# Attention scores from float32r parts in 48 and 50 rows, with TensorE's attention program written out

## The reference

```python
Q = (x @ Wq + bq)   # 32 heads of 16;  K, V: 8 heads of 16, each shared by 4 query heads
scores = einsum('bhqd,bhkd->bhqk', Q, K) / sqrt(16)
out = einsum('bhqk,bhkd->bhqd', softmax(scores), V)  @ Wo + bo
# moe: top 2 of 8 experts of 512x512 for each token, weights = softmax of the two gate logits
```

## Time and profile before

| | |
|---|---|
| median of 3 runs | 1973.47 us (1973.37 to 1979.02) |
| profiled execution: first to last instruction | 1974.0 us |
| profiled execution, own time | not given apart from the span; the span lies 0.5 us over the median |
| mean granted TensorE clock | 0.967 |
| TensorE (matmuls) busy | 1827.0 us, 93% |
| VectorE, ScalarE, GpSimd busy | 73%, 61%, 10% |
| rounds of attention | about 140 to 1632 us |

### The profile page before, as it was taken

The page is one execution under the profiler, slowest core; times in us unless marked ns, Lnnn a source line. Parts: engine busy times, 40 slices in busy tenths (PEclk is TensorE's granted clock), DMA queues, the critical chain, the costliest instruction groups (busy, mean ns, idle before and its releaser), DMA issues.

```text
span 1974.0 us, 35320 instructions
## 1 busy us (share of the span) xinstructions
PE 1827.0 (93%) x9850; PEld 684.5 (35%) x9851; DVE 1436.3 (73%) x1599; ACT 1203.5 (61%) x2291; POOL 204.3 (10%) x220
## 2 busy tenths in 40 slices
PE   6997999999999999999999999999999988857980
PEld 3532333333333333333333333333333216625870
DVE  4495888888888888888888888888888705562214
ACT  2334777777777777777777777777777783322330
POOL 4443120000000000000000000000000004051006
PEclk9998999999999999999999999999999998967995
DMA  5226330100100000001000100100000004034548
GB/s 180 82 74 113 130 113 18 33 11 14 32 11 11 11 32 11 11 11 32 11 11 18 33 11 14 32 3 3 3 24 3 25 4 151 1 133 149 165 138 255
DMA packets 77019, 104.49 MB, mean 53 GB/s; under 512 B 28072, under 2 KB 49592, under 8 KB 76992
## 3 DMA queue, kind: packets, MB, share of 16 engines
q1 hardware_dynamic: 62624, 61.37, 10.8%
q0 software_dynamic: 11920, 40.93, 6.0%
q10 hardware_dynamic: 2448, 1.84, 0.4%
HBM read 58.49 MB, written 45.22 MB: 53 GB/s over the span
## 4 chain that ended last, share of the span: by engine, by line
PE 87%; DVE 3%; POOL 3%; DMA 2%; issue 2%; ACT 1%; ACTq 0%; SPq 0%; DVEq 0%; POOLq 0%
PE bank L805 25%; PE bank L773 24%; PE bank L799 22%; PE bank L902 7%; PE bank L744 3%; DVE max_kc L1093 2%; DMA arena_q<-q_parts 1%; POOL slots_x L411 1%; PE bank L817 1%; PE bank L979 1%; POOL ys L420 1%; POOL xs L420 1%; PE bank L759 1%; ACT arena_p L639 1%; PE bank L929 1%
## 5 line engine op out<-in xcount | busy, mean ns | idle before, releaser
L1093 DVE TENSOR_REDUCE max_kc<-bank 128x1 f32<-128x1024 f32 x1024 | 1212.0, 1219 | 207.7 <-PE bank L773 201.2
L639 ACT ACTIVATE arena_p<-bank 128x512 f32<-128x512 f32 x2048 | 1057.5, 603 | 406.3 <-PE bank L799 402.4
L799 PE MATMUL bank<-arena_q,arena_k 99*128 (+1 forms) x2048 | 617.2, 379 | 22.1 <-DMA arena_q<-q_parts 14.0
L773 PE MATMUL bank<-arena_k,arena_q 96*128 (+1 forms) x2048 | 614.7, 381 | 3.4 <-DVE max_kc L1093 3.1
L805 PE MATMUL bank<-arena_p,v_cur 128*32 128x512 f32 x4096 | 546.0, 605 | 0.7 <-ACT arena_p L639 0.7
L773 PEld LDWEIGHTS bank<-arena_k,arena_q 96*128 (+1 forms) x2048 | 161.7, 97 | 501.4 <-issue 337.9
L799 PEld LDWEIGHTS bank<-arena_q,arena_k 99*128 (+1 forms) x2048 | 196.7, 97 | 394.0 <-ACT arena_p L639 159.4
L805 PEld LDWEIGHTS bank<-arena_p,v_cur 128*32 128x32 f32 x4096 | 80.6, 108 | 125.2 <-issue 109.9
L353 POOL COPY v_cur<-v_all 128x256 f32 (+1 forms) x8 | 3.2, 399 | 1159.3 <-PE bank L805 1159.2
L1245 DVE TENSOR_TENSOR x2T_lo<-bank,x2T_hi 128x512 fp32r<-128x512 f32 x39 | 27.0, 692 | 106.0 <-ACT x2T_hi L646 106.0
L744 PE MATMUL bank<-xT,arena_p 128*128 128x512 f32 x160 | 75.6, 594 | 2.8 <-ACT xT L587 2.8
(11 more groups left out here) (153 smaller groups left out, 883.0 us busy)
## 6 DMA issues: line engine op xcount, KB each, us to landing
arena_q<-q_parts SPq DMA_DIRECT2D x192, 64.0 KB, 2.3
slots_x<-be_sb POOLq DMA_DIRECT2D x39, 256.0 KB, 2.3
xs<-slots_x SPq DMA_DIRECT2D x39, 256.0 KB, 2.7
slots_y<-ys SPq DMA_DIRECT2D x39, 256.0 KB, 2.0
we_raw<-in_L_ffn_expert_w POOLq DMA_DIRECT2D x8, 1024.0 KB, 6.1
q_parts<-arena_k SPq DMA_DIRECT2D x16, 384.0 KB, 3.0
heads_out<-o_norm SPq DMA_DIRECT2D x33, 128.0 KB, 2.3
at<-heads_out SPq DMA_DIRECT2D x4, 1024.0 KB, 6.6
```

The costliest lines, as they stand in the source:

```text
L639: act.activation(probs[:, u % PRING, :], bank[:, ring_bank(("score", u)), :], ACT.Exp, scale=SCALE).then_inc(p_ready, 1)
L773: mm = pe.matmul(bank[:, 2 + 2 * (m % 2) + q, :], q_flat[0:CROW, bass.ds(qo, P)], k_flat[0:CROW, bass.ds((j // NC) * T + (2 * half + q) * ...
L799: pe.matmul(bank[:, ring_bank(("score", u)), :], k_flat[0:SROW, bass.ds((i // NC) * T + kt * P, P)], q_flat[0:SROW, bass.ds(qo, CH)], star ...
L1093: dve.reduce_max(max_kc[:, m:m + 1], bank[:, 2 + 2 * (m % 2):4 + 2 * (m % 2), :].rearrange("p a s -> p (a s)"), AX.X).then_inc(m_done, 1)
```

## The change

- **Two parts instead of three.** Queries and keys are split into two float32r parts (ScalarE the high one, GpSimd the low one with one subtraction). A score is three products (high-high, low-high, high-low) in 48 rows, and 50 with the ones and the shift, which has two parts too. The copies carry four bytes an element.
- **Slots.** 4 query slots and 4 key slots (KSLOTS); keys are loaded group by group, at the start for groups 0 to 3 and then when a group is done. TensorE waits for keys only where a new group begins (`j == NC` and later multiples). The ones are put down by four copies in the start phase.
- **Order in a step.** A maximum unit is split (`max_half`) and its halves stand between the scores: score, half, score, half, score, value product, half, score, half.
- **Shift.** `make_shift` has two operations instead of five, and both read the bank of the maxima; the second one signals neg_ready.
- **Loops.** TensorE's and SyncE's rounds are written out, without registers in the addresses. ScalarE's and VectorE's stay loops.
- The buffers xT, parts and qf get a place of their own; x_all shares the queries' place as before.

```diff
-    Q_PART = [0, 1, 2, 0, 1, 0]
-    K_PART = [0, 0, 0, 1, 1, 2]
-    SROW = CROW + 3
+    CROW = 3 * DK
+    ROWS = CROW + 2
+    NQD = NKD = 3
-    SLOTS = 8
+    SLOTS = 4
+    KSLOTS = 4
...
-        shift = sb("shift", [REP * TT, 3, P], BF16)
+        shift = sb("shift", [REP * TT, 2, P], F32R)
...
-            pool.memset(k_st[CROW:SROW, 0, :], 1.0).then_inc(ones_ready, 1)
+            for slot in range(KSLOTS):
+                pool.dma_start(k_st[CROW:ROWS, slot, :].rearrange("p (r s) -> p r s", s=P).bitcast(F32),
+                               ones[0:2, :].unsqueeze(1).to_broadcast([2, T // P, P])).then_inc(ones_ready, 16)
...
-                pool.tensor_tensor(qf[:, u, :], qf[:, u, :], parts[:, u, 0, :], ALU.subtract).then_inc(split_step, 1)
-                pool.wait_ge(split_step, 2 * p + 1)
-                pool.tensor_copy(parts[:, u, 1, :], qf[:, u, :]).then_inc(split_step, 1)
-                pool.wait_ge(split_step, 2 * p + 2)
-                pool.tensor_tensor(parts[:, u, 2, :], qf[:, u, :], parts[:, u, 1, :], ALU.subtract).then_inc(parts_ready, 1)
+                pool.tensor_tensor(parts[:, u, 1, :], qf[:, u, :], parts[:, u, 0, :].bitcast(F32),
+                                   ALU.subtract).then_inc(parts_ready, 1)
...
+            def load_keys(g, done):
+                src = [k_parts[a].rearrange("(g d) s -> g d s", d=DK)[g] for a in range(2)]
+                for row, a in ((0, 0), (DK, 0), (2 * DK, 1)):
+                    sp.dma_start(k_st[row:row + DK, g % KSLOTS, :].bitcast(F32), src[a]).then_inc(done, 16)
...
-            load_keys(slice(1, G), kr_dma)
-            load_queries(NC)
-            store_heads(0)
-            place_shift(1)
+            for g in range(1, KSLOTS):
+                load_keys(g, kr_dma)
+            for i in range(N - 2):
+                store_heads(i)
+                place_shift(i + 1)
+                if i + SLOTS < N:
+                    sp.wait_ge(s_full, UNITS * (i + 1))
+                    if i % NC == NC - 1 and i // NC + KSLOTS < G:
+                        load_keys(i // NC + KSLOTS, kr_dma)
+                        sp.wait_ge(kr_dma, 16 * NKD * (i // NC + KSLOTS))
+                    load_queries(i + SLOTS)
...
+            def max_half(j, m, q):
+                h, qt, half = m // (2 * TT), m // 2 % TT, m % 2
+                if q == 0:
+                    pe.wait_ge(m_done, MUNITS * j + m + 1)
+                return pe.matmul(bank[:, 2 + 2 * (m % 2) + q, :], q_st[0:CROW, j % SLOTS, h, qt * P:(qt + 1) * P],
+                                 k_st[0:CROW, j // NC % KSLOTS, (2 * half + q) * CH:(2 * half + q + 1) * CH],
+                                 start=True, stop=True)
...
                 if kt == SPLIT and with_max:
-                    pe.wait_ge(q_dma, 16 * NTERM * (j + 1))
-                    pe.wait_ge(kr_dma, 16 * NTERM)
-                    pe.wait_ge(ones_ready, 2)
+                    pe.wait_ge(q_dma, 16 * NQD * (j + 1))
+                    if j == NC:
+                        pe.wait_ge(kr_dma, 16 * NKD * (KSLOTS - 1))
+                    elif j % NC == 0 and j // NC >= KSLOTS:
+                        pe.wait_ge(kr_dma, 16 * NKD * (j // NC))
                 score_unit(i, REP * kt)
+                if with_max:
+                    max_half(j, m, 0)
                 score_unit(i, REP * kt + 1)
                 if with_max:
-                    max_unit(j, m)
+                    max_half(j, m, 1).then_inc(m_full, 1)
                 score_unit(i, REP * kt + 2)
...
                 if with_max:
-                    max_unit(j, m + 1)
+                    max_half(j, m + 1, 0)
                 score_unit(i, REP * kt + 3)
-            first_step(0)
-            with pe.Fori(0, N - 2) as i:
-                other_steps(i)
-                first_step(i + 1)
+                if with_max:
+                    max_half(j, m + 1, 1).then_inc(m_full, 1)
+            for i in range(N):
+                for kt in range(NKT):
                     attention_step(i, kt)
...
                 if part == 0:
                     dve.wait_ge(mT_full, j + 1)
-                    dve.wait_ge(shift_dma, 1 + 48 * j)
-                    dve.tensor_scalar(negmax[:, :], bank[0:REP * TT, B_MAX, 0:P], -1.0, None,
-                                      ALU.mult).then_inc(neg_ready, 1)
+                    dve.wait_ge(shift_dma, 1 + 32 * j)
+                    dve.tensor_scalar(shift[:, 0, :], maxima, -1.0, None, ALU.mult).then_inc(step_m, 1)
                 else:
+                    dve.wait_ge(step_m, j + 1)
+                    dve.scalar_tensor_tensor(shift[:, 1, :], maxima, -1.0, shift[:, 0, :].bitcast(F32),
+                                             ALU.mult, ALU.subtract).then_inc(neg_ready, 1)
...
-                        if 0 <= part < 5 and not last:
+                        if 0 <= part < 2 and not last:
                             make_shift(i + 1, part)
```

More of the change, by code:

```diff
@@ L148, in in_turn @@
             return made
-        with nc.sbuf_tensor("xT", [P, NC, KD, CH], F32) as xT:
-            pass
+        (xT, parts, qf), = in_turn(
+            [("xT", [P, NC, KD, CH], F32), ("parts", [P, 5, 2, CH], F32R), ("qf", [P, 5, CH], F32)])
         with nc.sbuf_tensor("we_raw", [P, E, KD, D], F32) as we_raw:
@@ L179, in preln_attention_moe @@
         ys = sb("ys", [P, SR, D])
-        (arena_q, arena_k, arena_p, v_all), = in_turn(
-            [("arena_q", [P, 8192], F32),
-             ("arena_k", [P, 8192], F32),
+        (x_all,), (q_st, k_st, arena_p, v_all) = in_turn(
+            [("x_all", [P, NKT, D], F32)],
+            [("q_st", [P, SLOTS, REP, CH], F32R),
+             ("k_st", [P, KSLOTS, T], F32R),
              ("arena_p", [P, 8192], F32),
@@ L449, in store_parts @@
                 sp.dma_start(dst[:, :, c * CH:(c + 1) * CH].rearrange("a p s -> p a s"),
[L450 to L455, removed]
+                             parts[:, u, :, :].bitcast(F32)).then_inc(parts_stored, 16)
@@ L464, in load_queries @@
-                wait_first(q_dma, 16 * NTERM * (j + 1))
+                src = [q_parts[a].rearrange("(f d) s -> d f s", d=DK)[:, g * REP:(g + 1) * REP, qc * CH:(qc + 1) * CH]
+                       for a in range(2)]
+                for row, a in ((0, 0), (DK, 1), (2 * DK, 0)):
+                    sp.dma_start(q_st[row:row + DK, slot, :, :].bitcast(F32), src[a]).then_inc(q_dma, 16)
+                sp.wait_ge(q_dma, 16 * NQD * (j + 1))
             def place_shift(j):
-                wait_first(shift_ready, j + 1)
@@ L468, in place_shift @@
-                for a in range(3):
-                    dst = q_st[CROW + a:CROW + a + 1, bass.ds(j % SLOTS, 1), :, :].squeeze(1)
+                sp.wait_ge(neg_ready, 1 + j + 1)
+                for a in range(2):
+                    dst = q_st[CROW + a:CROW + a + 1, j % SLOTS, :, :].bitcast(F32)
                     sp.dma_start(dst.rearrange("o h (t q) -> o (h t) q", t=TT),
-                                 shift[:, a, :]).then_inc(shift_dma, 16)
-                wait_first(shift_dma, 1 + 48 * (j + 1))
+                                 shift[:, a, :].bitcast(F32)).then_inc(shift_dma, 16)
@@ L474, in store_heads @@
+                sp.wait_ge(shift_dma, 1 + 32 * (j + 1))
             def store_heads(i):
@@ L765, in _ @@
                             projection_step(p, k)
-            def max_unit(j, m):
[L769 to L776, removed]
+            def max_half(j, m, q):
[5 more added lines that the diff above has]
+                                 start=True, stop=True)
+            def max_unit(j, m):
+                max_half(j, m, 0)
+                max_half(j, m, 1).then_inc(m_full, 1)
             def max_transpose(j):
@@ L797, in score_unit @@
                 ring_bank_free(i, ("score", u))
-                qo = (i % SLOTS) * (REP * CH) + h * CH
-                pe.matmul(bank[:, ring_bank(("score", u)), :], k_flat[0:SROW, bass.ds((i // NC) * T + kt * P, P)],
-                          q_flat[0:SROW, bass.ds(qo, CH)], start=True, stop=True).then_inc(s_full, 1)
+                pe.matmul(bank[:, ring_bank(("score", u)), :], k_st[0:ROWS, i // NC % KSLOTS, kt * P:(kt + 1) * P],
+                          q_st[0:ROWS, i % SLOTS, h, :], start=True, stop=True).then_inc(s_full, 1)
             def value_product(i, kt):
@@ L811, in output_transpose @@
                 pe.wait_ge(o_ready, i + 1)
-                if isinstance(i, int) and i == N:
+                if i == N:
                     pe.wait_ge(p_ready, len(SBANKS) + UNITS * N)
@@ L865, in attention_step @@
                     value_product(i, kt - 1)
-                elif not (isinstance(i, int) and i == 0):
+                elif i > 0:
                     value_product(i - 1, NKT - 1)
@@ L869, in attention_step @@
                     output_transpose(i)
-                if kt == MAX_T and not (isinstance(i, int) and i == N - 1):
+                if kt == MAX_T and i < N - 1:
```

(8 more changed lines are left out.)

72 lines of the change are left out of this document (13 added, 59 removed).

## The result

| | before | after |
|---|---|---|
| profiled execution, span | 1974.0 us | 2963.2 us (time 2964.8) |
| median of the runs | 1974.9 us (4 runs) | 3033.0 us (4 runs, 2964.8 to 3213.3) |
| mean granted TensorE clock | 0.967 | 0.659 |

The ratio is 1.504, with a 95% interval from 1.4995 to 1.5084. It compares the two shortest runs of the kernel after (2964.8 and 2976.9 us, clock 0.659 and 0.654) with the kernel before; the two others (3089 and 3213 us, clock 0.628 and 0.598) were longer, and their clock was lower. The forecast was 2092 us, 2038 to 2108: the sign was right, the size was off by a factor of eight (by the ratio some 995 us more, instead of 118).

The account below looks back on a forecast made before the run. TensorE's own program was taken as the bound, busy 93% of the run. Added costs 50 + 41 + 12 + 40 less savings 15.6, 5, 4 and 1 gave +118 us on 1974.0, so 2092 us, range 2038 to 2108.

Parts of the forecast that it names:

- The bank that is freed later: Score 45 waits for the maxima's bank, freed by the second shift operation: 1.34 us in 30 rounds, +40 us.
- The matmuls themselves: Score and maximum matmuls in float32r start 0.229 us apart, fewer rows saving nothing: 3912 x 0.0127, +50 us.
- Spacing: Score and maximum matmuls: float32r starts 0.229 us apart, 0.0127 more than bf16, 3912 times: +50 us.
- The first rival: Score and maximum matmuls: float32r with 48 rows keeps bf16's pace, so 2042 us; chance 0.13.
- two at a time: 48-row score and maximum matmuls overlap in pairs, leaving VectorE as the bound: near 1750 us; chance 0.04.
- Uncovered load: Behind value products the next float32r weight load isn't hidden: 427 x 0.097 us, +41 us.
- Change of shape: Returns from 128-row transposes to 48- or 50-row matmuls cost 0.2 us each, 63 times: +12 us.
- Bank wait: Score 45 waits 1.34 us for the maxima's bank in 30 rounds: +40 us.
- The second rival: VectorE's second shift operation frees the maxima's bank early enough, so score 45 doesn't wait: 2052 us; chance 0.09.
- Keys, loop, order: Savings: round 0's key wait and half clock -15.6, wait after output transposes -5, loop jumps -4, shift operations -1 us.
- the rival of code loading: TensorE's written-out program arrives late, adding a few us for each part of the code: over 2110 us; chance 0.06.
- The sum for the full clock: All terms for the whole kernel: +118 us on 1974.0, giving 2092 us.

Follow-up runs that it names:

- e7: Kernel after with 96 and 98 float32r rows and both shift operations one behind the other, so without the gap: 2056.6 us, ratio 1.043.
- e2: Kernel after, gap kept, but 96 and 98 float32r rows, filled with zeros beside the keys and copies beside the queries: 2099.1 us, ratio 1.0635.
- e1: Kernel after, but VectorE does both shift operations one behind the other, freeing the maxima's bank early: 2088.5 us profiled; others 2088.4, 2127.0, 2411.9.
- e4: Kernel before, 96 and 99 bf16 rows, with the five shift operations one reduction later, so TensorE waits once a round: 2013.8 us, ratio 1.0204.
- e8: Kernel before in bf16, plus TensorE's rounds written out, keys awaited where group 1 begins, and maximum halves between the scores: 1954.4 us, ratio 0.9911.
- e9: e1, but in VectorE's rounds 5, 13 and 21 the bank is freed late as in the kernel after: 2190.6 and 2268.6 us.
- e5: Kernel before, TensorE's rounds written out, three of six bf16 products (48 and 51 rows), shift operations one reduction later: 2205.4 and 2374.1 us.

## Why the prediction was wrong, and where it was right

**The step that failed** is in "The bank that is freed later": "TensorE stands for 1.34 us; behind it in its queue are the next maxima, the value product and so all scores, and as it is the bound it gets nothing back." The wait was found, its place and its length were right, and it was priced at its length and at the full clock. In its place: with 48 and 50 rows a gap of this length can put the granted clock from 1.00 to 0.50, and the rounds that follow run 1.8 times slower until it rises. By the estimate in the section on the result that is worth some 850 us here. e7 against e2 gives the price that I had assumed (42.5 us), e1 against the kernel after the one that held (876 us). The same assumption stands in "The matmuls themselves", which weighed fewer rows only by the pace of one matmul. None of the rivals had the clock in it, though the earlier trace rows already showed that it can be half for a while behind a hole.

The Trainium skill ("TensorE: Matmul & The Clock Gate", A second HAM failure mode: psum-queue depth-cycling) describes short idle times between groups of matmuls, from cycling through PSUM banks, that make the clock swing between its two levels. The trace of the kernel after agrees, with ten falls at waits for a bank of the ring, each about 1.04 us of idle time. But the waits alone didn't make the clock swing: it stayed at 1.00 through the same waits with 96 rows (e2, e4).

**The terms, at the full clock.**

- *Spacing* (+50): mis-sized. Measured 0.235 in e1 and the kernel after, not 0.229, so 3912 x 0.0185 = 72. The rows hardly matter to it: in e2's chain the 96-row ones take 0.23 to 0.24 too. The first rival falls with it, and so does that of two at a time.
- *Uncovered load* (+41): right. The first matmul is 0.50 long against 0.39 to 0.40, and the next one starts 0.34 behind it.
- *Change of shape* (+12): right, 0.42 against 0.23 (e1, e2).
- *Bank wait* (+40): right as the wait's own price, 42.5 (e7). The second rival, without this wait, falls.
- *Keys, loop, order* (-25): too large. e8 gives 1972.2 x 0.0089 = 17.5, with an interval of 14 to 21. The hole is gone, as windows show; loop and order gave some 4 instead of 9. e8's TensorE program is written out too, and its rounds got shorter, so the rival of code loading finds no support.
- The sum for the full clock, 2092, stands against 2088.5 for e1 plus e7's 42.5, 2131, for a kernel with the gap and no fall. Of the 39 us between them 23 are the spacing, about 5 the 11 us at half clock in the start phase, 7 or 8 the smaller savings and 2 or 3 the wait; that leaves next to nothing open.

**What stays open.** Why the clock fell behind the third gap of e9 and not behind the first two, and what lowered the clock in e1's two longer runs, no run here tells. Nor does any tell why the clock went back at some output transposes and not at others, or what float32r and the new order each add to the fall.

## What to carry to other kernels

A wait of TensorE isn't priced by its length alone. Look at how many rows the matmuls around it use: if they are as few as here, price the wait with the granted clock at one half for rounds behind it, or remove it. Where a matmul takes the same time with 48 rows as with 96, as here, the fuller one was the safer and the faster, even with zeros in the rows. When a read of a bank is split in two operations, put them behind each other on their engine, and the work that can wait behind both.

## What the runs showed of the hardware

- The rows in use changed TensorE's granted clock. With the same 1.42-us gap in each round its mean was 0.659 (48 rows), 0.78 to 0.81 (68) and 0.977 (96, half of them zeros beside the keys).
- In the rounds the falls came at the end of a gap or within 2 us behind it (the kernel after, e5, e9). The half clock lasted 44 to 410 us in the kernel after and 222 us of unbroken work in e9; it ended at the transposes of the outputs, 128 rows by 128 columns.
- Float32r matmuls of 512 columns started 0.235 us apart with 48 rows and 0.23 to 0.24 with 96, so more rows cost no time here. The same in bf16 is 0.215 to 0.217.
